# A retention kernel: the second head's attention output written to the opposite token half of its PSUM bank

## The reference, cut to what matters

```python
q = heads((x @ Wq + bq) * scaling); k = heads(x @ Wk + bk); v = heads(x @ Wv + bv)
D = jnp.where(causal[None], jnp.exp(decay[:, None, None] * diff_c[None]), 0.0)
ret = jnp.einsum('bhid,bhjd->bhij', q, k) * D[None]
scale = jnp.clip(jnp.abs(ret.sum(-1, keepdims=True)), 1.0, None)
attn = jnp.einsum('bhij,bhjd->bhid', ret / scale, v)
g = (g - mu) / jnp.sqrt(var + EPS)          # g: attn, statistics over each head's 64 features
g = g.reshape(b, s, e) * gn_w + gn_b
return jax.nn.silu(x @ Wg + bg) * g @ Wo + bo
```

## Time and profile before

| | |
|---|---|
| median of 3 runs | 2087.11 us (2085.61 to 2091.01) |
| the profiled execution's own time | 2089.4 us |
| its span, first to last instruction | 2087.2 us |
| TensorE busy | 2018.6 us, 97% of the span |
| VectorE busy | 1654.7 us, 79% |
| ScalarE busy | 693.0 us, 33% |
| GpSimd busy | 894.9 us, 43% |
| mean granted TensorE clock | 0.996 of full speed |

### The profile page before, as it was taken

One profiled execution on the slowest core, in us unless ns is written; L12 is line 12 of the kernel. 1 busy time (PEld: TensorE's weight loads), 2 busy tenths in 40 slices (PEclk: granted clock), 3 DMA queues, 4 the chain that ended last, 5 costly groups with the idle time before them and its releaser, 6 DMA issues.

```text
span 2087.2 us, 53514 instructions
## 1 busy us (share of the span) xinstructions
PE 2018.6 (97%) x18894; PEld 1114.6 (53%) x18894; DVE 1654.7 (79%) x4411; ACT 693.0 (33%) x1359; POOL 894.9 (43%) x634
## 2 busy tenths in 40 slices
PE   5899999999999999999999999999999999999999
PEld 3455545555555555555555555555555555555544
DVE  7677689998899898898988888877777877777832
ACT  5666522322232332223233323233323323322300
POOL 2233333332343343555544555544455554355520
PEclk9999999999999999999999999999999999999999
DMA  8899524333434434345435345435445434434542
GB/s 323 274 308 317 197 92 131 108 128 107 112 121 141 129 98 134 113 136 151 133 115 137 112 133 150 132 95 142 112 107 146 141 102 125 122 109 132 170 146 112
DMA packets 272090, 302.15 MB, mean 145 GB/s; under 512 B 204656, under 2 KB 205808, under 8 KB 271856
## 3 DMA queue, kind: packets, MB, share of 16 engines
q1 hardware_dynamic: 272000, 300.98, 47.9%
HBM read 207.33 MB, written 43.52 MB: 120 GB/s over the span
## 4 chain that ended last, share of the span: by engine, by line
PE 61%; DVE 30%; issue 5%; ACT 2%; DMA 1%; DVEq 0%; SPq 0%; POOL 0%; ACTq 0%; POOLq 0%
PE mm L1595 29%; PE mm L1612 9%; PE mm L1506 6%; PE tp L1506 6%; PE mm L1515 3%; PE four L1670 2%; DVE xa L1087 2%; DVE gst L1326 2%; DVE state L1312 2%; PE four L1683 2%; DVE xa L1082 2%; DVE xa L1095 1%; DVE xa L1094 1%; DVE xm L1089 1%; DVE wo L1200 1%
## 5 line engine op out<-in xcount | busy, mean ns | idle before, releaser
L1595 PE MATMUL mm<-xnT,wring 128*128 128x512 f16 x4776 | 1069.6, 380 | 12.8 <-ACT qT L856 5.1
L1595 PEld LDWEIGHTS mm<-xnT,wring 128*128 128x128 f16 x4776 | 458.8, 98 | 547.1 <-issue 14.2
L1612 PE MATMUL mm<-wring,xnT 128*128 128x256 f16 x2688 | 302.8, 273 | 5.6 <-DVE res L1455 5.3
L1612 PEld LDWEIGHTS mm<-wring,xnT 128*128 128x128 f16 x2688 | 261.4, 98 | 50.9 <-DVE res L1455 14.8
L918 ACT ACTIVATE work<-four,gs 128x64 f32<-128x64 f32 x512 | 158.1, 414 | 374.5 <-DVE gs L1339 374.5
L685 POOL TENSOR_TENSOR yT<-gn,gate 128x512 f32 (+1 forms) x64 | 87.8, 1371 | 339.1 <-ACT gn L929 230.0
L1506 PE MATMUL mm<-wo,yT 128*128 128x512 f16 x960 | 215.5, 381 | 4.1 <-POOL yT L690 3.7
L662 POOL TENSOR_TENSOR qparts<-qT,qparts 128x512 f16<-128x512 f32 x64 | 78.8, 1232 | 247.3 <-ACT qT L856 247.3
L698 POOL TENSOR_TENSOR nparts<-work,nparts 128x512 f16<-128x512 f32 x41 | 47.4, 1156 | 263.6 <-ACT nparts L904 263.6
L1326 DVE BATCH_NORM_STATS2 gst<-four 128x6 f32<-128x64 f32 x512 | 73.3, 215 | 100.2 <-PE four L1683 98.7
L1506 PEld LDWEIGHTS mm<-wo,yT 128*128 (+1 forms) x960 | 91.2, 98 | 113.3 <-POOL yT L690 4.2
(11 more groups left out here) (226 smaller groups left out, 3000.4 us busy)
## 6 DMA issues: line engine op xcount, KB each, us to landing
wring<-parts SPq DMA_DIRECT2D x252, 512.0 KB, 4.3
xt<-in_x SPq DMA_DIRECT2D x34, 512.0 KB, 4.7
out<-res SPq DMA_DIRECT2D x32, 512.0 KB, 3.0
parts<-wo SPq DMA_DIRECT2D x28, 512.0 KB, 5.9
res<-in_x SPq DMA_DIRECT2D x28, 512.0 KB, 3.7
ftile<-in_w_f SPq DMA_DIRECT2D x12, 512.0 KB, 4.8
parts<-wring SPq DMA_DIRECT2D x8, 512.0 KB, 8.4
probs<-in_x SPq DMA_DIRECT2D x5, 512.0 KB, 5.0
```

The costliest lines, as they stand in the source:

```text
L1595: last = MM(mm[n % 2][:], wring[:, slot, wj, k, :], xnT[:, parity, xj, k, :], start=(k == 0 and j == 0), stop=(k == KT - 1 and j == 2))
L1612: last = MM(out[:, c], xnT[:, parity, xj, k, tokens], wring[:, 1::2, wj, k, :], start=(n == 0), stop=(n == 3 * KT - 1))
```

## The change

The first head of a pair keeps its place in its bank. The second head's block k goes to the other token half: `places(k, h)` is `tokens(k)` for h = 0 and the opposite half for h = 1. Both attend functions write there. For the second head, `normalize` then reads each half of the partitions on its own and writes it to the opposite half of `work`, with the scale and bias of the partitions it reads, so that `work` is as before. So there are four products of 128 partitions and eight of 64 in place of eight of 128. `group_norm` is unchanged: its statistics are per partition.

```diff
                     for c in range(CH):
                         for h in range(2):
                             g = h * CH + c
-                            last = nc.scalar.activation(
-                                work[:, c * P + h * HD:c * P + (h + 1) * HD], ao[h][:, c * VW:c * VW + HD],
-                                ACT.Identity, bias=gs[:, 1, g:g + 1], scale=gs[:, 4, g:g + 1])
+                            features, columns = slice(c * P + h * HD, c * P + (h + 1) * HD), slice(c * VW, c * VW + HD)
+                            for out, rows in (((0, P),) * 2,) if h == 0 else (((0, SUB), (SUB, P)), ((SUB, P), (0, SUB))):
+                                out, rows = slice(*out), slice(*rows)
+                                last = nc.scalar.activation(work[out, features], ao[h][rows, columns], ACT.Identity,
+                                                            bias=gs[rows, 1, g:g + 1], scale=gs[rows, 4, g:g + 1])
                     last.then_inc(s["normed"], 1)
...
                 tokens = lambda k: slice(k % 2 * SUB, (k % 2 + 1) * SUB)
+                places = lambda k, h: tokens(k ^ h)
                 columns = lambda k: slice(k // 2 * VW, (k // 2 + 1) * VW)
...
-                            last = MM(ao[h][tokens(k), columns(k)], probs[tokens(k), h, k // 2, 0:SUB],
+                            last = MM(ao[h][places(k, h), columns(k)], probs[tokens(k), h, k // 2, 0:SUB],
                                       v1[tokens(k), k // 2, v_head(u, h), :], start=(k < 2), stop=False, skip_group_check=True)
...
-                            last = MM(ao[h][tokens(k), columns(k)], qT[r, u, k * SUB:(k + 1) * SUB], state[r, k],
+                            last = MM(ao[h][places(k, h), columns(k)], qT[r, u, k * SUB:(k + 1) * SUB], state[r, k],
                                       start=False, stop=True, skip_group_check=True)
```

## The result

The changed kernel takes 2183.03 us (median; 2175.53 to 2184.74), the kernel before, run beside it, 2086.91 (2085.61 to 2091.01): a ratio of 1.045, 95% interval 1.0436 to 1.0465. It is slower, as forecast, but by 96 us where 13.4 were forecast; 2183 lies far above the range that ended at 2114.

A forecast was written before the change was run, and what follows sets the result against it. TensorE, 97% busy, was taken to bound the steady passes, VectorE groups two and three. Terms 2.9 + 2.8 + 2.0 + 4.2 + 0 + 1.5 = +13.4 took 2089.4 to 2102.8, less 2.3: 2100.5 us, range 2082 to 2114.

The forecast's parts named there:

- TensorE's part: L1670's sixteen products go round four quarters, saving 0.51 us a block, 32.6 us over 32 passes if all counted.
- that case: Rival that half-high products cost half, so normalize grows no longer: -12, 2075 us; chance 0.10.
- The rival of quarters that take turns: Two row halves writing one bank cost turns, so L1670 stays at 1.08 us: +28, 2115 us; chance 0.08.
- ScalarE's part: Four more products in normalize at 0.294 us each, 1.18 us per normalize; bounds 0 and 1.65.
- The sign named for it: L918's normalize blocks under 3 us or over 4 would show the forecast wrong; 3.65 us was expected.
- What waits for it: Step following the 1.18 us longer normalize to the gate's copy, L1515, GpSimd's gating and the second group norm.
- passes 6 to 12: VectorE holds the chain, L1670's saving is hidden, second normalize delays L1635: 0.6 us a pass, +4.2.
- passes 22 to 31: TensorE saves 0.51 and 0.11, a longer second group norm costs 0.91: +0.29 us a pass, +2.9 for ten.
- passes 13 to 20: VectorE's ring gains 0.10 of delay, group norm grows 1.01: +0.4 us a pass in 14 to 20; +3.8 with pass 13.
- The opening: Little spare before L1670 and L1534, but other waits take up the loss: 0 us, between -2 and +3.
- the tail: The last pair's gating chain grows by 1.18 and about 1 of stalled group norm, less 0.7: +1.5 us.
- The rival without overlap: Products of 64 partitions in normalize don't overlap, 1.65 us more a block: +29, 2116 us; chance 0.10.

The follow-up runs named there:

- with eight products: The changed kernel with its TensorE part kept but normalize back to eight full-height products (second head's token halves stay exchanged in the output): 2074.02 us, ratio 0.9934.
- with twelve: The run with eight products, with the second head's four products made once more at full height into unused columns, in both pairs: 2126.90 us, ratio 1.0183.
- with twelve in the first pair: Twelve full-height products in the first pair's normalize of each pass, eight in the second's, otherwise as with eight products: 2096.29 us, ratio 1.0047.
- with twelve in the second pair: Twelve full-height products in the second pair's normalize of each pass, eight in the first's, otherwise as with eight products: 2109.10 us, ratio 1.0097.
- inside a group: The changed kernel with normalize's products reordered: first head's four, four from upper to lower half, four from lower to upper: 2142.55 us, ratio 1.0259.

## Why the prediction was wrong

**TensorE's part** was right: 0.65 to 0.70 a block was asked for, and a block that doesn't wait takes 0.65; with eight products the whole came to 2074.0, forecast 2075 for that case. The rival of quarters that take turns is out: in these blocks two row halves write one bank, each its own partitions, and no cost of it shows.

**ScalarE's part is the step that failed first**: "I take 0.294 each, since the columns are the same: 1.18 us for each `normalize`". It is 2.50 (4.97 - 2.47). Not even the upper end, 1.65, was one: it let only the four added products lose their overlap, while the row from which 0.294 came showed products that all begin at the same partition. A full product between two halves that begin elsewhere loses it too. The sign named for it, blocks over 4 us, is what the trace shows. The lost overlap makes 56 us of the 83 by which the forecast was short. The Trainium skill (ScalarE: Activation LUTs, What ACT_TABLE_LOAD costs) gives back-to-back operations an overlap of some 93 ns without a condition. The runs here differ from that: an operation of 0.41 us that is followed after 0.29 overlaps its neighbour by about 0.12 where both first partitions stay, and not at all where either changes.

**"What waits for it" failed second.** With blocks of 3.66 the forecast's 2100.5 should have come; 2126.9 came, outside the range as well. The text follows `normalize(0)` through passes 13 to 31 and prices `normalize(1)` only in passes 6 to 12 and at the end. The first was right in the 23rd pass, each term within 0.13 us, and near in passes 22 to 31; in passes 13 to 20 its sum was right by luck. The second pair costs 35 us alone. In the profiled executions it is 38.0, of which 16.7 lie in passes 13 to 20 and 8.7 in 21 to 31, where it was left at nothing. The opening (0, measured +0.2 with twelve) and passes 6 to 12 (+4.2, measured +2.2) were near, and the tail was off by under 2 us (+1.5, measured +3.2); passes 13 to 20 (+3.8, measured +20.9) and 21 to 31 (+3.9, measured +10.7) were not. A slip of rounding beside this costs half a microsecond: 1.18 - 0.40 - 0.51 is 0.27 and not 0.2, so that the term for passes 6 to 12 should read +4.7.

**In the changed kernel** both faults meet: 2.50 more uses up the 1.54 between the end of `normalize` (1423.75) and the second L1670 block (1426.37 less 1.08), and L1673 itself waits: 0.96 by this, 0.93 in the trace; passes 5 to 12, where L1536 stands straight behind `normalize`, lose 31 us. The chain of the second pair has a smaller part here than with twelve overlapping products: over the whole span L1686 waits 14.0 us for the carry, there 27.9, with eight 13.5. The lower clock is a term that the sum doesn't have. **The sign** was the forecast's. The rival without overlap was the nearest, but at 1.65 a block and with the same followers left out it gave 2116.

## What to carry to other kernels

A price per instruction read from a row holds for that row's neighbours: check what the next instruction must share with it, here the first partition on both sides, and put instructions that share it next to each other (that alone brought 2183 to 2143). And when something is delayed that occurs twice in a loop, follow each occurrence to its last user; the one at the end of the loop delays the next turn. Where two engines block each other such a delay can grow: 1.2 us cost 0.9 a pass on the chain that was followed (61.10 with eight to 62.03 with twelve in the first pair, 23rd pass) and 2.8 where it set VectorE's operations beside GpSimd's (61.51 to 64.28 with twelve in the second pair, 15th pass).

## What the runs showed of the hardware that was not expected

Neighbouring ScalarE operations on 64 columns follow each other by 0.29 to 0.30 us when both read and both write from the same first partition, also from a full height to a half, and by 0.40 to 0.42 when the first partition changes on the reading or on the writing side. Moving data between token halves costs nothing by itself (0.29 inside a group). An operation of 64 partitions lasts as long as one of 128 (401 and 405 ns).

In the 23rd pass with twelve products in the second pair, VectorE's state copy started after GpSimd's L730 and ended with it, 2.33 us for an operation whose median is 0.20. The Trainium skill (SBUF — State Buffer, Who interferes with whom) says that a copy can take the pair of ports shared with GpSimd, and that the engine that comes second then waits out the other's instruction; the ends, 0.05 us apart, agree.
